# Softmax numerators of every other pair on ScalarE in two batches, mixing tiles of 25 tokens, and an emptier last drain

## The chip, the cores and the metric

One Trainium2 chip, one of its cores. The metric is device time in microseconds of one execution of the kernel; less is better. The numbers of the profile come from one profiled execution of the same kernel.

## The reference

Sixteen batches of x (256 channels, 2048 positions) and a context of the same shape, all in fp32. First a linear attention across channels, then a hyper-connection block; both add to x.

```
qh = softmax over the 64 of each head (Wq @ layernorm(x)) * SCALE       # 8 heads of 64
kh = softmax over positions (Wk @ ctx);  vh = Wv @ ctx
out = Wo @ ((kh @ vh^T)^T @ qh) + bo
x  = x + out / norm(out) * g * sqrt(DIM)

logits = rms_norm(layernorm(x)) @ [W_res, W_pre, W_post]^T + base       # per token, 16 + 4 + 4
H_res  = sinkhorn(logits_res, 50 iterations, tau 0.1), mixed with the identity by a gate
H_pre, H_post = softmax(...)
y = (sum of the 4 streams by H_pre) @ W_branch
x = x + H_res applied to the 4 streams of 512 columns + H_post * y
```

A token is one of the 256 channels of a batch, 2048 wide, cut into four streams of 512.

## The kernel before

Five engines run programs written out by hand, with semaphores. A batch b has a **key stage**, 32 places ("A" or "B", b, r, i) for four blocks r of 128 key rows and four quarters i of the positions, and a **query stage**, places ("Q", b, i) with i from 0 to 26 (STEPS = 27). The query stage works on 16 tiles of 128 positions, in 8 pairs. PE makes a tile's logits in `big[i % 2]` (`query_logits`, L675 to L677); DVE takes each head's maximum (`query_max`, L949) and subtracts it into `q_sb` (`query_subtract`, L959); two steps later ScalarE takes the exponential of the pair (`query_exp`, L1259), POOL adds the halves of each head (`query_half`, L1507, into `x_pre`), DVE sums them and takes the reciprocal (`query_sum`, L967 and L971), and POOL normalises (`query_normalise`, L1515). PE transposes (`query_transpose`, L686, into one of two banks `tb`), ScalarE copies (`turn`, L1254, into one of three `turned`), PE multiplies (`attention_out`, L701). Squares of the result (ScalarE, L1270), its norm (POOL, L1525 and L1528), the scaling (DVE, L980) and the addition to x (POOL, L1535) follow; PE returns the pair to rows (`return_pair`, L720, and the maps of the second block's logits, L723), ScalarE copies the rows (`rows_of_pair`, L1277), DVE takes statistics (L889). `query_logits` of tile i+2 waits until tile i has been read out of `big` (`s_qsub`). Steps 16 to 26 are the drain: no logits of that batch are left, and where another batch follows, its first key logits are made there. Behind the last batch stands one place TAIL.

A **planner** at the top of the file puts further tasks at these places. The batches form five groups (2, 4, 4, 4, 2). When a group's logits are there, its Sinkhorn iteration runs in 116 steps ("sink"), of some three small DVE operations each (L1055 to L1063) with ScalarE's exponentials and logarithms (L1341) between some of them; each step is put at one of the free places of the following batches. For group 3 fewer places than steps are left, so that many places get two. Then the coefficients go to DRAM, and the group's tokens are **mixed** in tiles of TOK = 24 tokens: SP loads 5 rows of 512 columns a token (four streams and y, `mix_ld`, L544), the coefficients (`mix_co`, L546) and biases (L548); POOL (in the last group DVE) builds a block matrix (`mix_w`, L1497, L1133); PE multiplies (L757, two matmul records a tile); ScalarE copies out (`mix_bank`, L1322, two buffers `mix_out`), SP stores 4 rows a token (L554). Loads run four tiles ahead (AHEAD), and one tile is put at every third place (PACE) from the time that its group is ready. What is left goes to TAIL, between the steps of the last group's iteration, and behind that the last group's own tiles, while its last 256 tokens are computed from SBUF (`own`, L1327, L1149, stored by L560 in eight transfers of 128 rows). On each engine, a task waits behind everything put before it.

## Time and profile before

| | |
|---|---|
| median of 3 runs | 2565.55 us (2563.75 to 2566.59) |
| profiled execution | 2568.32 us |
| its span, first to last instruction | 2566.6 us |
| mean granted TensorE clock | 0.982 |
| PE, DVE, ACT, POOL busy | 2413.9, 1726.8, 1172.8, 1094.4 us |
| DMA | 255.72 MB, 100 GB/s in the mean |

In the rows below, engines are PE (TensorE's matmuls), PEld (its weight loads), DVE, ACT (ScalarE), POOL (GpSimd) and SP, which issues the DMAs. A row of a group of instructions has: line, engine, operation, output<-inputs, output shape<-input shape, xcount | busy us, mean ns of one | idle time of the engine just before them and what ended it. Batch 15's query stage begins at 2320.6 us with its first logits, its last logits at 2381.7; the iteration of the last group begins at 2426.8.

### The profile page before, as it was taken

What the parts mean: (1) busy time and instruction counts of PE and PEld (TensorE: products, weight loads), DVE (VectorE), ACT (ScalarE), POOL (GpSimd) and SP (SyncE); (2) the same over time, 40 slices, a digit from 0 to 9 for tenths busy, and PEclk for the clock granted to TensorE, in tenths of its full rate; (3) what the DMA queues carried; (4) which work ended last, traced back from release to release, by engine and by line L of the source; (5) the groups of instructions that cost most, each with busy time, mean ns of one, the idle gap of its engine ahead of it and who ended that gap; (6) DMA issues with size and microseconds to landing.
All of it is one profiled execution on the core that took longest, in us unless ns stands there. A gap on an engine that the chain in (4) does not pass through costs nothing.

```text
span 2566.6 us, 35379 instructions
## 1 busy us (share of the span) xinstructions
PE 2413.9 (94%) x12004; PEld 1914.3 (75%) x12004; DVE 1726.8 (67%) x4114; ACT 1172.8 (46%) x2464; POOL 1094.4 (43%) x1107
## 2 busy tenths in 40 slices
PE   7999999999999999999999999999999999899774
PEld 6888878887878778787877778777778876777521
DVE  4454567676767557776776567667687756877786
ACT  4454444545354444545444454544445344453333
POOL 1635536172635427262543616245272633623410
PEclk9999999999999999999999999999999999999887
DMA  7112221313122432312213243343302233231376
GB/s 237 50 66 99 74 92 56 108 41 103 63 70 96 128 119 83 113 62 70 95 67 99 80 153 93 120 141 101 123 34 90 92 114 117 76 117 44 88 221 193
DMA packets 200145, 255.72 MB, mean 100 GB/s; under 512 B 43550, under 2 KB 109854, under 8 KB 199966
## 3 DMA queue, kind: packets, MB, share of 16 engines
q1 hardware_dynamic: 199966, 253.47, 31.3%
q8 instruction: 96, 1.57, 0.3%
q14 instruction: 83, 0.68, 0.1%
HBM read 177.53 MB, written 75.89 MB: 99 GB/s over the span
## 4 chain that ended last, share of the span: by engine, by line
PE 57%; DVE 20%; POOL 11%; issue 8%; ACT 3%; SPq 1%; DMA 1%; DVEq 0%; POOLq 0%; ACTq 0%
PE kc_bank L642 15%; PE big L701 7%; PE tb L743 4%; PE tb L757 3%; PE tb L628 3%; PE big L616 3%; PE big L618 3%; PE big L617 3%; POOL x_tr L1535 3%; DVE stats L889 3%; PE big L675 3%; PE big L677 2%; PE big L676 2%; PE tb L686 2%; POOL q_sb L1515 2%
## 5 line engine op out<-in xcount | busy, mean ns | idle before, releaser
L1254 ACT COPY turned<-tb 128x512 f32<-128x512 f32 x512 | 298.7, 587 | 755.3 <-PE tb L686 487.9
L701 PE MATMUL big<-merged,turned 128*128 128x256 f32 x2048 | 495.0, 385 | 36.3 <-ACT turned L1254 24.5
L642 PE MATMUL kc_bank<-ctxt,turned 128*128 128x256 f32 x2048 | 479.5, 380 | 3.0 <-DMA ctxt<-in_ctx_t 3.0
L701 PEld LDWEIGHTS big<-merged,turned 128*128 128x128 f32 x2048 | 385.8, 191 | 110.7 <-ACT turned L1254 19.4
L642 PEld LDWEIGHTS kc_bank<-ctxt,turned 128*128 128x128 f32 x2048 | 374.6, 191 | 54.6 <-issue 8.9
L1490 POOL TENSOR_TENSOR in_l<-x_sb,in_h 128x512 fp32r<-128x512 f32 x128 | 167.8, 1340 | 574.9 <-ACT in_h L1294 574.8
L1515 POOL TENSOR_TENSOR q_sb<-q_sb,qsum 128x1024 f32<-128x1024 f32 x128 | 243.8, 1904 | 274.4 <-DVE qsum L971 274.4
L980 DVE SCALAR_TENSOR_TENSOR on<-big,nrm,g_rows 128x256 f32<-128x256 f32 x256 | 111.9, 479 | 220.7 <-POOL nrm L1528 220.4
L616 PE MATMUL big<-in_h,wk_h 128*128 128x512 f32 x512 | 237.7, 464 | 15.4 <-DVE in_l L821 10.0
L675 PE MATMUL big<-wq_h,in_h 128*128 128x512 f32 x512 | 236.4, 462 | 10.9 <-DVE q_sb L959 10.4
L757 PE MATMUL tb<-mix_ld,mix_w 121*96 121x512 f32 (+2 forms) x324 | 187.9, 677 | 57.7 <-POOL mix_w L1497 28.0
L949 DVE TENSOR_REDUCE qmax<-big 128x8 f32<-128x512 f32 x256 | 176.3, 689 | 93.1 <-PE big L677 88.5
L862 DVE TENSOR_REDUCE kmax<-big 128x1 f32<-128x512 f32 x256 | 172.4, 686 | 91.9 <-PE big L618 88.6
L617 PE MATMUL big<-in_l,wk_h 128*128 128x512 f32 x512 | 203.8, 398 | 0.0
L618 PE MATMUL big<-in_h,wk_l 128*128 128x512 f32 x512 | 203.6, 398 | 0.0
L677 PE MATMUL big<-wq_h,in_l 128*128 128x512 f32 x512 | 202.2, 395 | 0.0
L676 PE MATMUL big<-wq_l,in_h 128*128 128x512 f32 x512 | 201.9, 394 | 0.0
L1322 ACT COPY mix_out<-tb 96x512 f32<-96x512 f32 (+2 forms) x162 | 94.0, 580 | 234.4 <-PE tb L757 189.5
L1245 ACT ACTIVATE k_exp<-big,kmax 128x512 f32<-128x512 f32 x256 | 175.4, 689 | 35.5 <-DVE kmax L869 35.4
L959 DVE TENSOR_TENSOR q_sb<-big,qmax 128x512 f32<-128x512 f32 x256 | 169.4, 662 | 28.4 <-PE tb L686 25.8
L889 DVE BATCH_NORM_STATS2 stats<-x_sb 128x6 f32<-128x512 f32 x256 | 163.5, 681 | 35.4 <-ACT x_sb L1277 28.8
L1507 POOL TENSOR_TENSOR x_pre<-q_sb 128x512 f32<-128x512 f32 x128 | 163.0, 1273 | 50.3 <-ACT q_sb L1259 50.1
(149 smaller groups left out, 4308.5 us busy)
## 6 DMA issues: line engine op xcount, KB each, us to landing
mix_ld<-streams SPq DMA_DIRECT2D x157, 240.0 KB
ctxt<-in_ctx_t SPq DMA_DIRECT2D x64, 512.0 KB, 4.0
x_sb<-in_x SPq DMA_DIRECT2D x64, 512.0 KB, 6.1
x_tr<-in_x_t SPq DMA_DIRECT2D x64, 512.0 KB, 6.6
streams<-x_sb SPq DMA_DIRECT2D x64, 512.0 KB, 3.1
stage<-in_ctx SPq DMA_DIRECT2D x60, 512.0 KB, 4.1
out<-mix_out SPq DMA_DIRECT2D x157, 192.0 KB, 2.2
streams<-y_sb SPq DMA_DIRECT2D x32, 256.0 KB, 2.0
```

The source lines that it names most:

```text
L616: nc.tensor.matmul(big[i], wk_h[:, ct, cols], in_h[:, ct, quarter(i)], start=ct == 0, stop=False)
L617: nc.tensor.matmul(big[i], wk_h[:, ct, cols], in_l[:, ct, quarter(i)], start=False, stop=False)
L618: t = nc.tensor.matmul(big[i], wk_l[:, ct, cols], in_h[:, ct, quarter(i)], start=False, stop=ct == CT - 1)
L642: t = nc.tensor.matmul(kc_bank[:, 0:C], turned[n % 3][:, j * P:(j + 1) * P], ctxt[:, nt, :], start=nt == 0, stop=nt == NT - 1)
L675: nc.tensor.matmul(big[i % 2], in_h[:, ct, at], wq_h[:, ct, :], start=ct == 0, stop=False)
L676: nc.tensor.matmul(big[i % 2], in_h[:, ct, at], wq_l[:, ct, :], start=False, stop=False)
L677: t = nc.tensor.matmul(big[i % 2], in_l[:, ct, at], wq_h[:, ct, :], start=False, stop=ct == CT - 1)
L701: t = nc.tensor.matmul(big[2 + p % 2][:, half], turned[n % 3][:, dt * P:(dt + 1) * P], merged[:, dt, :], start=dt == 0, stop=dt == DT - 1)
L757: t = nc.tensor.matmul(bank[0:count * STREAMS, :], weights, mix_ld[k][0:ONES + 1, :], start=True, stop=True)
L889: t = nc.vector.bn_stats(target[:, ct, i, :], x_sb[b % 2][:, ct, quarter(i)])
L1254: nc.scalar.copy(turned[k % 3][:], tb[n % 2][:]).then_inc(s_tba, 1)
L1515: nc.gpsimd.tensor_tensor(exps, exps, qsum[:, p % 2, 1, :].unsqueeze(2).broadcast_to([P, 2 * HEADS, DIM_HEAD]), ALU.mult).then_inc(s_qn, 1)
```

## The change

- SCALAR_PAIRS marks every second pair (1, 3, 5, 7) of batches 14 and 15. For these DVE writes the negated maximum (`qneg`), there is no subtraction, no `query_exp` and no `query_half`. Instead ScalarE's `query_soft` takes, head by head, the exponential of 64 columns straight from `big` with the maximum as bias and the sum as accumulator output, in the step of the tile itself. Waits are rewritten to count the two kinds of pairs.
- TOK is 25, so tiles have 125 and 100 rows.
- Group 3's iteration may not use places behind step 11 of batch 15.
- No mixing tile is put at steps 14 and later of batch 15.
- In steps 16 and later of batch 15 PE transposes a tile before `attention_out` of the one ahead of it, not behind it.

```diff
-    TOK = 24
+    TOK = 25
     PARTS = STREAMS + 1
...
     for gr in range(LAST):
-        free = [place for place in order_of_places[starts[gr]:starts[gr + 1] - 8]
+        free = [place for place in order_of_places[starts[gr]:starts[gr + 1] - (8 if gr < LAST - 1 else STEPS - 12)]
                 if place[0] == "Q" and 5 <= place[2] < NT + 4 or place[0] == "B" and (place[2] >= 2 or place[2:] > (1, 1))
...
             since = min(since, PACE - 6)
-        if place[0] != "Q" and place[2] == 0:
+        if place[0] != "Q" and place[2] == 0 or place[:2] == ("Q", NB - 1) and place[2] >= NT - 2:
             continue
...
     use_tb_behind(TAIL)
+    SCALAR_PAIRS = [b >= FIRST[-1] and k % 2 == 1 for b in range(NB) for k in range(PAIRS)]
+    def scalar_pairs(n):
+        return sum(SCALAR_PAIRS[:n])
+    def vector_pairs(n):
+        return n - scalar_pairs(n)
+    def sums_done(n):
+        return 2 * (n + 1) - scalar_pairs(n + 1)
...
         qmax = sb("qmax", [P, 2, HEADS])
+        qneg = sb("qneg", [P, 2, HEADS])
         qhalf = x_pre[:].rearrange("p (h d) -> p h d", d=DIM_HEAD // 2)
...
             return ap.bitcast(F32)
+        def wait_tile(w, m):
+            n = m // 2
+            if SCALAR_PAIRS[n]:
+                w.wait_ge(s_qacc, 2 * scalar_pairs(n) + m % 2 + 1)
+            else:
+                w.wait_ge(s_qsub, 2 * vector_pairs(n) + m % 2 + 1)
...
                     if b and i < 2:
-                        w.wait_ge(s_qsub, (b - 1) * NT + NT - 1 + i)
+                        wait_tile(w, b * NT - 2 + i)
                     elif b:
...
                 if i >= 2:
-                    w.wait_ge(s_qsub, n - 1)
+                    wait_tile(w, n - 2)
                 else:
...
                         key_context(b, DT - 1, 2 * i + 1)
+                    first = b == NB - 1 and i >= NT
+                    if 4 <= i < NT + 4 and first:
+                        query_transpose(b, i - 4)
                     if 5 <= i < NT + 5:
...
                         return_pair(b, (i - 10) // 2)
-                    if 4 <= i < NT + 4:
+                    if 4 <= i < NT + 4 and not first:
                         query_transpose(b, i - 4)
...
                 w.wait_ge(s_ql, b * NT + i + 1)
+                n = b * PAIRS + i // 2
+                if SCALAR_PAIRS[n]:
+                    w.wait_ge(s_qacc, 2 * scalar_pairs(n))
+                    nc.vector.tensor_reduce(qneg[:, i % 2, :], big[i % 2].rearrange(heads, d=DIM_HEAD), AX_X,
+                                            ALU.max, negate=True).then_inc(s_qmax, 1)
+                    return
                 nc.vector.tensor_reduce(qmax[:, i % 2, :], big[i % 2].rearrange(heads, d=DIM_HEAD), AX_X,
...
                 p = b * PAIRS + i // 2
+                if SCALAR_PAIRS[p]:
+                    return
                 w.wait_ge(s_qmax, n + 1)
...
                 n = b * PAIRS + p
-                w.wait_ge(s_half, n + 1)
-                nc.vector.tensor_reduce(qsum[:, p % 2, 0, :], qhalf, AX_X, ALU.add).then_inc(s_qsum, 1)
-                w.wait_ge(s_qsum, 2 * n + 1)
+                if SCALAR_PAIRS[n]:
+                    w.wait_ge(s_qacc, 2 * scalar_pairs(n + 1))
+                else:
+                    w.wait_ge(s_half, vector_pairs(n + 1))
+                    nc.vector.tensor_reduce(qsum[:, p % 2, 0, :], qhalf, AX_X, ALU.add).then_inc(s_qsum, 1)
+                    w.wait_ge(s_qsum, sums_done(n) - 1)
                 if n >= 2:
...
                 n = b * PAIRS + p
-                w.wait_ge(s_qsub, 2 * n + 2)
+                w.wait_ge(s_qsub, 2 * vector_pairs(n + 1))
                 nc.scalar.activation(q_sb[n % QB][:], q_sb[n % QB][:], ACT.Exp).then_inc(s_qexp, 1)
+            def query_soft(b, i):
+                p, j = i // 2, i % 2
+                n = b * PAIRS + p
+                w.wait_ge(s_qmax, b * NT + i + 1)
+                if p >= QB or b:
+                    last = (n - QB) * 2 + 1
+                    w.wait_ge(s_tb, TB["fg", last // NT * FG + DT * NQ + last % NT] + 1)
+                if n >= 2:
+                    w.wait_ge(s_qsum, sums_done(n - 2))
+                for h in range(HEADS):
+                    cols = slice(h * DIM_HEAD, (h + 1) * DIM_HEAD)
+                    k = j * HEADS + h
+                    t = nc.scalar.activation(q_sb[n % QB][:, j, cols], big[j][:, cols], ACT.Exp, bias=qneg[:, j, h:h + 1],
+                                             accum_out=qsum[:, p % 2, 0, k:k + 1])
+                t.then_inc(s_qacc, 1)
...
                         turn(b * FG + DT * NQ - 1)
-                    if i >= 2 and i % 2 == 0 and i < NT + 2:
+                    if i < NT and SCALAR_PAIRS[b * PAIRS + i // 2]:
+                        query_soft(b, i)
+                    if i >= 2 and i % 2 == 0 and i < NT + 2 and not SCALAR_PAIRS[b * PAIRS + (i - 2) // 2]:
                         query_exp(b, (i - 2) // 2)
...
                 exps = q_sb[n % QB].rearrange("p t (h d) -> p (t h) d", d=DIM_HEAD)
-                w.wait_ge(s_qexp, n + 1)
+                w.wait_ge(s_qexp, vector_pairs(n + 1))
                 if n:
-                    w.wait_ge(s_qsum, 2 * n - 1)
+                    w.wait_ge(s_qsum, sums_done(n - 1))
                 nc.gpsimd.tensor_tensor(qhalf, exps[:, :, 0:DIM_HEAD // 2], exps[:, :, DIM_HEAD // 2:DIM_HEAD],
...
                 exps = q_sb[n % QB].rearrange("p t (h d) -> p (t h) d", d=DIM_HEAD)
-                w.wait_ge(s_qsum, 2 * n + 2)
-                w.wait_ge(s_half, n + 1)
+                w.wait_ge(s_qsum, sums_done(n))
+                w.wait_ge(s_half, vector_pairs(n + 1))
                 nc.gpsimd.tensor_tensor(exps, exps,
...
                         query_normalise(b, (i - 3) // 2)
-                    if i >= 2 and i % 2 == 0 and i < NT + 2:
+                    if i >= 2 and i % 2 == 0 and i < NT + 2 and not SCALAR_PAIRS[b * PAIRS + (i - 2) // 2]:
                         query_half(b, (i - 2) // 2)
```

## Rows read from the trace of the kernel before

**Rows 1.** The page, busy time: us (share of the span) xinstructions.

```profile
PE 2413.9 (94%) x12004; PEld 1914.3 (75%) x12004; DVE 1726.8 (67%) x4114; ACT 1172.8 (46%) x2464; POOL 1094.4 (43%) x1107
```

**Rows 2.** Stretches: keys 10, 14; queries 11, 14, 15; drain 15; iteration; the rest.

```profile
core 0: us, PE busy (x) PEld busy (x) DVE busy (x) ACT busy (x) POOL busy (x), PEclk, DMA share, GB/s
1434.90:1534.10 99.20, 95.08 (x478) 73.75 (x475) 54.94 (x140) 52.44 (x114) 37.82 (x46) 1.00 0.44 136
2045.60:2152.10 106.50, 96.69 (x476) 73.27 (x475) 68.43 (x182) 53.27 (x118) 37.05 (x46) 1.00 0.39 122
1690.40:1748.20 57.80, 57.19 (x287) 46.89 (x286) 40.92 (x78) 23.80 (x48) 34.96 (x32) 1.00 0.33 99
2152.10:2214.70 62.60, 58.73 (x288) 46.82 (x286) 48.49 (x99) 23.79 (x45) 31.77 (x30) 1.00 0.34 103
2320.60:2381.70 61.10, 58.93 (x288) 46.89 (x286) 46.70 (x96) 21.68 (x46) 26.66 (x26) 1.00 0.17 50
2381.70:2426.80 45.10, 35.23 (x167) 26.51 (x168) 29.77 (x69) 14.51 (x37) 23.13 (x29) 0.82 0.23 67
2426.80:2527.90 101.10, 72.55 (x122) 19.35 (x120) 81.50 (x341) 36.55 (x83) 16.58 (x46) 0.82 0.75 212
2527.90:2566.60 38.70, 14.79 (x22) 4.08 (x22) 24.21 (x46) 12.63 (x21) 0.00 (x0) 0.68 0.64 182
```

**Rows 3.** The chain of waits inside batch 15's query stage: start us, us, what.

```profile
by line: DVE skw L1061 16.5%; DVE skw L1055 14.7%; DVE q_sb L959 13.8%; DVE qmax L949 11.0%; issue 7.2%; PE big L675 5.7%; DVE skb L1063 5.6%; DVE ska L1057 5.6%; DVE qsum L967 5.3%; DVE skr L1056 4.6%; DVE skr L1062 4.6%; PE big L677 3.7%;
...
2353.25 1.60 DVE skw L1061
```

**Rows 4.** Groups of instructions by line, the whole span.

```profile
L757 PE MATMUL tb<-mix_ld,mix_w 121*96 121x512 f32 (+2 forms) x324 | 187.9, 677 | 57.7 <-POOL mix_w L1497 28.0 <-DVE mix_w L1133 17.8 <-ACT mix_out L1322 8.0
...
L959 DVE TENSOR_TENSOR q_sb<-big,qmax 128x512 f32<-128x512 f32 x256 | 169.4, 662 | 28.4 <-PE tb L686 25.8
...
L1259 ACT ACTIVATE q_sb<-q_sb 128x1024 f32<-128x1024 f32 x128 | 135.7, 1060 | 104.0 <-DVE q_sb L959 103.9
...
L1270 ACT ACTIVATE squares<-big 128x256 bf16<-128x256 f32 x256 | 98.3, 384 | 24.6 <-PE big L701 20.5
...
L967 DVE TENSOR_REDUCE qsum<-x_pre 128x16 f32<-128x512 f32 x128 | 86.9, 679 | 14.6 <-POOL x_pre L1507 14.3
...
L1270 ACT ACTIVATION_READ_ACCUMULATOR squares<-big 128x1 f32 x256 | 50.6, 198 | 0.0
...
L1341 ACT ACTIVATE skr<-ska 128x32 f32<-128x32 f32 (+1 forms) x25 | 5.7, 226 | 22.1 <-DVE skb L1063 22.1
```

**Rows 5.** The chain of waits at the end of batch 15's drain.

```profile
2419.30 1.84 PE tb L757 x2
...
2421.65 0.59 ACT x_sb L1277
```

**Rows 6.** DMA packets in 2338:2346 us, then in 1012:1020 us with issues.

```profile
DMA packets 384, 0.44 MB, mean 56 GB/s; under 512 B 168, under 2 KB 168, under 8 KB 384
...
DMA packets 487, 0.82 MB, mean 103 GB/s; under 512 B 94, under 2 KB 94, under 8 KB 486
...
streams<-x_sb SPq DMA_DIRECT2D x1, 512.0 KB, 2.9
...
mix_ld<-streams SPq DMA_DIRECT2D x1, 80.0 KB
```

**Rows 7.** DMA packets and issues in the tail, 2480:2520 us.

```profile
DMA packets 8321, 9.83 MB, mean 246 GB/s; under 512 B 3557, under 2 KB 3557, under 8 KB 8318
...
q1 hardware_dynamic: 8318, 9.80, 86.5%
...
mix_ld<-streams SPq DMA_DIRECT2D x21, 240.0 KB
```

**Rows 8.** DMA packets in 2340.87:2341.19 us, one engine at work.

```profile
DMA packets 5, 0.01 MB, mean 26 GB/s; under 512 B 1, under 2 KB 1, under 8 KB 5
```

**Rows 9.** ScalarE in the tail, in order of time.

```profile
2496.97 0.58 ACT L1322 COPY mix_out<-tb 96x512 f32<-96x512 f32 x1 [1.28 <-DMA out<-mix_out]
```

More of the change, by code:

```diff
@@ L293, in xattn_ffn @@
         s_qsub = sem("s_qsub")
+        s_qacc = sem("s_qacc")
         s_qexp = sem("s_qexp")
```

## The prediction, before the changed kernel was run

> **What bounds the kernel now.** I read the page's busy times first: PE is busy for 94% of the span [rows 1], so most of the kernel is a matter of what PE is given to do. Then the stretches by stage [rows 2], where the reader is to compare like with like. The query stage of batch 11 takes 57.8 us with PE busy for 57.2 of them; those of batches 14 and 15, with the same PE instructions to within one, take 62.6 and 61.1 us. What differs is DVE: 48.5 and 46.7 us busy against 40.9. The chain of waits inside batch 15 runs through DVE for most of its length, Sinkhorn products ahead of all, one of them at 1.60 us [rows 3]. So there DVE sets the pace. The drain of batch 15 (45.1 us) is a mixture, and its last link is a mixing tile: ScalarE's copy of the returned rows comes behind a matmul of L757 [rows 5]. From there to the end of the iteration of the last group (101.1 us) two things run side by side. DVE is busy for 81.5 us; the DMA engines are busy for 75%, and at 86.5% in the stretch of [rows 7], where 40 us hold 21 tile loads, so 1.9 us a tile. ScalarE's copy out waits there for the DMA of two tiles before [rows 9]. That stretch is bound by DVE and by the transfers at once, which matters for what follows. The last 38.7 us are transfers and the eleven last tiles.
>
> **Mixing tiles of 25: count.** Groups of 512, 1024 and 256 tokens give 22, 43, 43, 43 and 11 tiles of 24, and 21, 41, 41, 41 and 11 of 25: 155 instead of 162. Followed through the planner, three of the seven saved lie in key stages (one in batch 7, two in batch 12), three in the last batch, and one behind the last batch (49 instead of 50 under the last group's iteration). A tile's two matmuls cost PE 0.86 us at the full clock in the chain (their 677 ns each [rows 4] overlap): -2.6 us for the three.
>
> **Mixing tiles of 25: the transfers.** A load has 5 rows of 2 KB a token, 120 before and 125 after, a store 4 rows a token, 96 and 100. How rows are shared out is to be read from the small packets. In the first stretch of [rows 6] one store of 96 rows, one load of 120, one load of 120 coefficient rows and one bias row leave 168 packets under 512 B: 120 coefficients, 1 bias, and 47 others. In the second the load has 40 rows (80 KB): 94 small packets, less 40 and 1 leaves 53, with a spill of 128-row form beside it. Taken as one closing packet from each DMA engine that took part, 47 is 16+15+15+1 and 53 is 16+16+10+10+1. So 96 rows went over 16 engines, 120 over 15, 40 over 10: each time the largest number up to 16 that divides the rows. 125 is 5x5x5, so I forecast five engines for each load, and ten for a store of 100 rows. The Trainium skill, in DMA: Bandwidth & Descriptors, section "Why a DMA increments its semaphore by 16 and not by 1", states that very rule for the engine count, and also that such a transfer goes to the lowest-numbered engines; the trace agrees on the counts (47 and 53), and no row shows which engines. This speaks against the change.
>
> The price. On its own, one DMA engine moved four 2 KB packets in 0.32 us [rows 8], 0.080 us each. In the loaded tail 8318-3557 = 4761 large packets kept 86.5% of 16 engines busy over 40 us, 0.116 us each with all small ones put on them [rows 7]. An engine that takes part in both has 8+6 = 14 large packets a tile now, 1.1 to 1.6 us of the 1.9. With the change the busiest five have 25+10 = 35: 2.8 us at the lower price, 4.1 at the upper. I take 0.095 us, 3.3 us a tile, since what makes a packet dearer than 0.080 comes in part once a transfer, and a transfer now has more packets. 49 tiles: 163 us, against 101.1 us: **+62 us** (137 to 201: +36 to +100). DVE's iteration is hidden behind it, but its last ScalarE functions are queued behind the copies out of all 49 tiles, so the last group's coefficients come that much later. In the last 38.7 us the eleven tiles put about 11x35x0.095 = 37 us on the busiest engines and the eight stores of the last tokens (128 rows, 8 packets each) 6 us more, from the first load, which comes once the coefficients are stored, some 5 us in by my estimate: 48 to 50 us, **+11 us** (+5 to +21).
>
> Before the last batch a tile comes every third place, some 12 us apart (57.8 us for 15 places [rows 2]), and is loaded four tiles ahead, so 35 packets (3.3 us) an engine are covered; only other loads queued behind four first loads of a group (10 us) can be late. I take +2 us (0 to +8).
>
> **Every other pair by ScalarE.** In batches 14 and 15 four pairs each lose on DVE two subtractions of 662 ns and one sum of 679 ns [rows 4], 2.0 us, and on POOL a half sum. ScalarE loses one exponential of 1.06 us and gains sixteen of 64 columns with sixteen accumulator reads of 198 ns. Nearest rows for the former: 226 ns for 32 columns, 384 for 256. So a head costs from 0.20 us (the activation hidden under the read) to 0.58, and I take 0.226+0.198 = 0.43, since 64 is nearest to 32: 3.4 us a tile, 6.9 a pair. ScalarE is busy for 23.8 of 62.6 us in this stage [rows 2], 3 us a pair of about 9: with 5.8 more it has 9 in such a pair and 3 in the next. It fits, but not freely. The exponential of the pair before is now queued behind the first tile's eight heads, so POOL's half sum and DVE's next sum come some 3 us later: I estimate 1.5 us of the 2.0 saved are lost to that wait. What is next late is PE, whose floor for the stage is batch 11's 57.8 us: at most -4.8 and -3.3 us.
>
> **The iteration of group 3** has 116 steps; its places end at step 11 of batch 15 instead of 18. So batch 14 gets 35 instead of 31 in its key stage and 32 instead of 28 in its query stage, batch 15 gets 34 instead of 31 and then 15 instead of 28. In key stages 15 more steps cost 106.5-99.2 = 7.3 us [rows 2], 0.49 each: 7 more, +3.5 us (0 to +7; DVE is busy 13.5 us more for the 15 steps, 0.9 a step). In batch 14's query stage four more steps eat what DVE is saved: -1 us (-4.8 to +5); in batch 15's -2 us (-3.3 to +4).
>
> **The last drain.** Thirteen steps at 0.9 us leave DVE, three mixing tiles leave PE, and a transpose goes ahead of the product that waits for ScalarE's copy of the transpose before. In all but one short stretch after the last product the order of PE sets the end. The link through L757 goes wholly: the rows can be copied when PE is done with the maps, at 2419.3 instead of 2421.65 [rows 5], 2.3 us. PE is idle for 10 of the 45.1 us and runs at 0.82 of its clock, its lower level for part of it [rows 2]. I take -8 us (0 to -13).
>
> **Sum**, against the profiled execution of 2568.3 us (span 2566.6, 1.7 around it): -2.6 +62 +11 +2 +3.5 -1 -2 -8 = +65. The median of the runs is 2.8 us under the profiled one: 2565.55+65 = **2630 us**. All lower ends together give about +15, all upper ones about +140.
>
> **Rivals.** (1) The transfers spread evenly after all, since 125 rows are shared some other way or each transfer starts at another engine. For it: no row shows a number without a divisor between 6 and 16, nor which engines are used. Against: 15 for 120 and 10 for 40 are what divisors give, and an even share would have given 16 and 14 or more. A tile then costs as now, one tile less lies in the tail, and -2.6+3.5-1-2-8 = -10 remains: **2555 us**, faster. It decides as soon as the busiest engine has fewer than 1.9/0.095 = 20 packets a tile. (2) The same, with ScalarE as the bound of the two query stages: at 0.7 us a head (the 0.58 above and a wait of 0.12) a pair would be 11 us on top of 2, against 9 of PE: +4 us on eight pairs, 2555+35 = **2590 us**. For it: accumulator reads are separate instructions; against: durations of neighbours on one engine mostly overlap, and it takes the far end of the price. (3) The five engines bind, but at their floor of 0.080 us and with the drain at its best: still about 2582 us, part of the forecast.
>
> **How the numbers follow.** Forecast 0.86, rival 1 0.09, rival 2 alone 0.05. Of the forecast only its lowest corner could be under +0.2% (what a measurement can tell apart here is about 0.2%, 5 us): 0.01. Slower 0.85+0.04 = 0.89, same 0.01+0.01+0.01 = 0.03, faster 0.08. The range leaves rival 1 out (0.09) and a few hundredths at each end of the forecast: 2592 to 2685 us.
>
> **What would show it.** In the tail, GB/s falls from 246 to near 130 to 150, with the DMA share near half; ScalarE's and POOL's waits for DMA grow; DVE, now over 80% busy there, falls to near 50%. A step with one tile has 16-byte packets 125 instead of 120 and 10+5+5+1 = 21 closing packets. Query stages of 14 and 15 near 60 us; copies of rows in the last drain without a mixing copy ahead. The prediction is wrong if the tail's 49 tiles still pass at 1.9 us each.

## The result

The changed kernel takes 2614.2 us (median, 2613.8 to 2614.5), the kernel before beside it 2564.65 us: ratio 1.0191, interval 1.0175 to 1.0207. It is 49.6 us slower. The forecast was 2630 us, with a range of 2592 to 2685.

The page of the kernel after: busy times, and the last three rows of the 40 slices (65.3 us each).

```profile
PE 2431.3 (93%) x11990; PEld 1915.5 (73%) x11990; DVE 1703.7 (65%) x4090; ACT 1200.0 (46%) x2705; POOL 1083.6 (41%) x1092
...
PEclk9999999999999999999999999999999999999655
DMA  7112122213132342213123442433212342311444
GB/s 233 57 62 101 65 97 73 89 46 112 46 100 79 121 140 96 89 41 113 49 67 97 129 140 87 150 92 103 93 65 97 102 131 85 115 50 44 145 158 156
```

PE is busy for 93% (94% before), and for 17 us more in all. In the last three slices the granted clock is 0.6, 0.5 and 0.5 of full speed, and the DMA share is 0.4 to 0.5. PE at a low clock and partly idle, the DMA engines more than half idle, and yet the stretch is long: something narrow sets it.

The stretches of the kernel after that answer to [rows 2]: the query stage of batch 14, the stretch to batch 15's, its query stage, its drain, the last group's iteration, the rest.

```profile
core 0: us, PE busy (x) PEld busy (x) DVE busy (x) ACT busy (x) POOL busy (x), PEclk, DMA share, GB/s
...
2147.40:2212.40 65.00, 59.07 (x288) 46.67 (x287) 43.09 (x93) 34.91 (x141) 28.61 (x27) 1.00 0.30 93
2212.40:2325.30 112.90, 98.89 (x480) 75.03 (x478) 87.87 (x235) 57.13 (x148) 37.55 (x46) 0.98 0.28 89
2325.30:2390.40 65.10, 59.11 (x288) 46.62 (x287) 38.99 (x90) 32.03 (x138) 25.62 (x25) 1.00 0.16 44
2390.40:2425.10 34.70, 28.37 (x164) 23.60 (x163) 12.74 (x32) 16.51 (x62) 18.11 (x23) 0.90 0.16 57
2425.10:2568.00 142.90, 94.28 (x120) 23.42 (x118) 81.82 (x344) 37.02 (x82) 16.77 (x45) 0.60 0.45 154
2568.00:2612.50 44.50, 19.82 (x22) 4.67 (x22) 23.93 (x44) 12.19 (x19) 0.00 (x0) 0.57 0.47 159
```

| stretch | before | after | difference |
|---|---|---|---|
| up to batch 14's query stage | 2152.1 | 2147.4 | -4.7 |
| query stage of batch 14 | 62.6 | 65.0 | +2.4 |
| from there to batch 15's query stage | 105.9 | 112.9 | +7.0 |
| query stage of batch 15 | 61.1 | 65.1 | +4.0 |
| drain of batch 15 | 45.1 | 34.7 | -10.4 |
| iteration and rest | 139.8 | 187.4 | +47.6 |

The differences sum to +45.9, that of the spans. The before column is worked out from [rows 2] and the times between them; 105.9 is 2320.6 less 2214.7. The iteration and the rest stand together here, since their border is an operation's end; by the end of DVE's last coefficient operation they are 101.8 and 38.0 before, 142.9 and 44.5 after. The reader is to see in the iteration's row that DVE is busy for the same 82 us as before, ScalarE for the same 37, and that the DMA share fell from 0.75 to 0.45: only PE is busy for longer, at a clock of 0.60 instead of 0.82, and by the chain below it does not set the end (its matmuls of tiles are 5.2% of that chain).

The chain of waits of the kernel after, from the start of the iteration to the end (2425 to 2612 us): its shares by line, and three of its pieces (start us, us, what).

```profile
by line: DMA out<-mix_out 62.4%; ACT mix_out L1377 8.2%; DMA mix_w<-bias_rows 7.1%; PE tb L781 5.2%; DVE k_exp L1187 5.2%; issue 2.7%; SPq L570 1.4%; SPq L572 1.0%; SPq L568 0.6%; ACT k_exp L1382 0.4%; ACT skp L1396 0.4%; SPq L578 0.4%; DVE
...
2442.16 0.59 ACT mix_out L1377
2442.77 4.89 DMA out<-mix_out
2447.74 0.59 ACT mix_out L1377
```

62% of the chain is stores of mixed tiles on their way, 4.89 us in the piece shown. Under the iteration ScalarE waits 41 times for such a store, 89.2 us in all; in the kernel before it was 28 times and 33.8 us, of which [rows 9] shows one. From a copy over its store to the next copy but one, which needs the same buffer, it is 5.6 us for two tiles here, and 142.9 us for 49 in the mean, 2.92 each.

### The profile page after: what moved, and what is told of

It reads as the page before. It is cut to its first block, busy times and chain, and to the rows that moved or that the text cites. A ratio compares the mean times of both kernels' runs of the same rounds, so it can differ in the third digit from the quotient of the medians.

```text
span 2612.5 us, 35500 instructions
## 1 busy us (share of the span) xinstructions
PE 2431.3 (93%) x11990; PEld 1915.5 (73%) x11990; DVE 1703.7 (65%) x4090; ACT 1200.0 (46%) x2705; POOL 1083.6 (41%) x1092
## 4 chain that ended last, share of the span: by engine, by line
PE 56%; DVE 16%; POOL 10%; issue 7%; DMA 5%; ACT 4%; SPq 1%; POOLq 0%; DVEq 0%; ACTq 0%
PE kc_bank L666 15%; PE big L725 8%; DMA out<-mix_out 4%; PE tb L767 4%; PE tb L652 3%; PE big L640 3%; PE big L642 3%; PE big L641 3%; PE tb L781 3%; POOL x_tr L1592 3%; DVE stats L916 2%; PE big L699 2%; PE big L701 2%; PE big L700 2%; PE tb L710 2%
## 5 line engine op out<-in xcount | busy, mean ns | idle before, releaser
L781 PE MATMUL tb<-mix_ld,mix_w 126*100 126x512 f32 (+2 forms) x310 | 206.3, 759 | 82.8 <-POOL mix_w L1554 51.5
L982 DVE TENSOR_REDUCE qmax<-big 128x8 f32<-128x512 f32 x240 | 165.0, 688 | 95.0 <-PE big L701 90.8
L1377 ACT COPY mix_out<-tb 100x512 f32<-100x512 f32 (+1 forms) x155 | 90.9, 587 | 265.3 <-PE tb L781 157.9
L1564 POOL TENSOR_TENSOR x_pre<-q_sb 128x512 f32<-128x512 f32 x120 | 152.7, 1273 | 84.7 <-ACT q_sb L1297 84.5
L1592 POOL TENSOR_TENSOR x_tr<-x_tr,on 128x512 f32<-128x512 f32 x128 | 164.9, 1288 | 39.7 <-DVE on L1018 39.7
```

Of the source, the lines that this page charges most:

```text
L781: t = nc.tensor.matmul(bank[0:count * STREAMS, :], weights, mix_ld[k][0:ONES + 1, :], start=True, stop=True)
L1592: nc.gpsimd.tensor_tensor(pair, pair, on[:], ALU.add).then_inc(s_sum, 1)
```

## How the transfers are shared out

One tile in the body of the kernel after, 2343:2351 us, which answers to [rows 6].

```profile
GB/s 0 0 0 0 143 102 113 113 143 174 102 92 82 123 133 123 133 123 133 123 133 123 67 35 42 0 1 0 0 0 0 0 0 0 0 0 0 0 0 0
DMA packets 373, 0.47 MB, mean 59 GB/s; under 512 B 147, under 2 KB 147, under 8 KB 372
...
mix_ld<-streams SPq DMA_DIRECT2D x1, 250.0 KB
```

147 packets under 512 B: 125 coefficient rows, one bias row, and 21 others. Read as closing packets, 21 is 10 for the store of 100 rows, 5 for the load, 5 for the coefficients and 1 for the bias row. That is what the divisors gave. With the load alone at work the rate is 123 to 133 GB/s in slice after slice (0.2 us each), five times the 26 GB/s of one engine in [rows 8].

### Tiles of 25 and nothing else: e1_tok25

```diff
-    TOK = 24
+    TOK = 25
```

> The kernel before with tiles of 25 tokens and nothing else. Theory 1 (a load of 125 rows goes over five DMA engines, 25+10 packets of 2 KB a tile on the busiest): the 50 or so tiles behind the last batch pass at 2.9 us each as in the changed kernel, against 1.9; the iteration of the last group takes about 143 to 150 us instead of 101, the end 6 us more, so 2608 to 2618 us in all, nearly the whole of what the change cost. Rival (the slower tail comes from the other edits, which leave more to do there): within 10 us of the kernel before.

Measured: 2603.86 us, ratio 1.0138 (1.0123 to 1.0153). The iteration and the rest:

```profile
2418.30:2554.70 136.40, 88.44 (x114) 21.57 (x112) 81.75 (x344) 35.24 (x79) 15.99 (x43) 0.61 0.45 153
2554.70:2599.70 45.00, 18.98 (x22) 4.28 (x22) 23.88 (x44) 12.19 (x19) 0.00 (x0) 0.62 0.47 158
```

136.4+45.0 = 181.4 us instead of 139.8, so 41.6 us of the changed kernel's 47.6. The iteration and the total are 7 and 4 us under the ranges I had written: with the old planning only 46 tiles are left for the iteration, not 49, and 46 at 2.97 us is 136.4. The other three are those that the changed kernel takes out of the last batch. The loss of the tail comes with this one number; the rival falls.

### Five rows apart: e5_split_load

The changed kernel; a tile's semaphore is waited for at 64 instead of 48.

```diff
-                nc.sync.dma_start(mix_ld[k][0:count * PARTS, :], streams[tokens].rearrange("c s n -> (c s) n")).then_inc(
-                    s_mixld[k], 16)
+                for part in (slice(0, count - 1), slice(count - 1, count)):
+                    nc.sync.dma_start(mix_ld[k][part.start * PARTS:part.stop * PARTS, :],
+                                      streams[first + part.start:first + part.stop].rearrange("c s n -> (c s) n")
+                                      ).then_inc(s_mixld[k], 16)
```

> The changed kernel, tiles of 25, but each tile's load is issued as two DMAs: the rows of all its tokens but the last (120 rows) and those of the last (5 rows). Same bytes, one issue more a tile. Theory 1 (engines are shared out by divisors of the rows, always from the same end): 8+1 rows of the load and 10 of the store, 19 packets at most an engine instead of 35, 1.6 us, so that SP's five issues a tile (1.9 us) or DVE's iteration set the pace: the last iteration takes 100 to 108 us instead of 142.9, 2565 to 2578 us in all. Rival (tiles of 25 are slow in the tail for another reason: more bytes in one load, 25 columns blocks for POOL, waits in SP): 135 us or more, and no faster than the changed kernel.

Measured: 2578.09 us, ratio 1.0045 (1.0032 to 1.0059), 36 us under the changed kernel for the same bytes. The iteration:

```profile
2427.00:2538.00 111.00, 78.37 (x120) 20.00 (x118) 82.26 (x344) 36.52 (x81) 16.48 (x45) 0.76 0.68 197
```

111.0 us, 2.27 a tile, 3 us over the upper end I gave; the total is at its upper end. One tile's issues on SP in that kernel, from a store to the next:

```profile
2494.38 0.29 SPq L580 DMA_DIRECT2D out<-mix_out  x1
2494.71 0.68 SPq L569 DMA_DIRECT2D mix_ld<-streams  x2
2495.44 0.42 SPq L572 DMA_DIRECT2D mix_co<-coef_rows  x1
2495.91 0.48 SPq L574 DMA_DIRECT2D mix_w<-bias_rows  x1
2496.43 0.29 SPq L580 DMA_DIRECT2D out<-mix_out  x1
```

SP is taken for 2.05 us a tile by five issues. I had put them at 1.9. That is close to the 2.27, but SP still waits 25.7 us in this stretch for ScalarE's copies, so it does not set the pace alone; what sets the rest was not tried. That the load on five engines was the cause is shown: the same rows as 120 and 5 pass in 111.0 us, as 125 in 142.9.

### Tiles of 23: e6_tok23

```diff
-    TOK = 24
+    TOK = 23
```

> The kernel before with tiles of 23 tokens and nothing else: 115 rows in (divisors 5 and 23) and 92 out (4 and 23). 54 tiles under the last iteration instead of 50. Theory 1 (fixed engines, from the same end): 23+23 = 46 packets a tile on the busiest four, at 0.083 us 3.8 us a tile; the iteration takes 195 to 215 us, the kernel 2670 to 2700. Theory 1b (the divisor rule, but loads and stores on different engines): 23 packets, 1.9 us a tile, 103 to 112 us, 2570 to 2585. Rival (a tile's size decides, and 23 is smaller than 24): as before, within 12 us.

Measured: 2686.95 us (one execution with its profile), 121 us over the kernel before, by a tile that is one token smaller. The iteration:

```profile
2429.10:2629.20 200.10, 110.75 (x130) 24.32 (x128) 81.48 (x344) 39.41 (x87) 17.87 (x51) 0.55 0.32 112
```

200.1 us for 54 tiles, 3.71 us a tile; with 23+23 packets that is 0.081 us a packet. This run was chosen for the question that no row before could answer: which engines. 115 rows go over five and 92 over four: one tile in its body (2340 to 2348 us) leaves 131 packets under 512 B, 115 coefficients, one bias row and 15 others, which are 5+4+5+1. Had loads and stores used different ones, or another set each time, the busiest would have had 23 packets or fewer and the iteration some 105 us, by an estimate from 1.9 us a tile. So both go to the same ones each time. The Trainium skill says the same in DMA: Bandwidth & Descriptors, section "Why a DMA increments its semaphore by 16 and not by 1": the lowest-numbered engines. The runs agree in that the sets overlap (46 packets at 0.081 us, not 23); that they are the lowest is not shown here.

Four kernels side by side, with the busiest engine's packets of 2 KB a tile:

| kernel | packets | us a tile | us a packet |
|---|---|---|---|
| before, tiles of 24 | 8+6 = 14 | 1.9 | 0.14 (not the limit alone) |
| e5, 120+5 in, 100 out | 8+1+10 = 19 | 2.27 | 0.12 (not the limit alone) |
| after, 125 in, 100 out | 25+10 = 35 | 2.92 | 0.083 |
| e6, 115 in, 92 out | 23+23 = 46 | 3.71 | 0.081 |

The last two have nearly the price of an engine on its own, 0.080 us [rows 8]; e1, with the same 35 packets, has 2.97 us a tile and 0.085.

## What the other edits do

### All but the tile size: e2_after_tok24

```diff
-    TOK = 25
+    TOK = 24
```

against the changed kernel.

> The changed kernel with tiles of 24 tokens. Theory 1: the iteration is back at about 102 us and the rest at 38; what stays is the query stages and the key stage of the last two batches (+1 +2 +7 +4 us) against the drain (-10), so 2566 to 2572 us. Rival (the edits themselves weigh on the tail, since the tiles taken out of the last batch have to be mixed there): iteration over 108 us, total over 2578.

Measured: 2572.81 us, ratio 1.0021 (1.0012 to 1.0031). The same stretches but the first and the last (batch 14's queries, to batch 15's, its queries, drain, iteration):

```profile
2149.10:2214.10 65.00, 60.11 (x288) 48.00 (x287) 43.14 (x93) 34.86 (x141) 28.61 (x27) 0.97 0.31 96
2214.10:2329.80 115.70, 101.73 (x478) 77.18 (x477) 87.84 (x235) 56.96 (x148) 37.33 (x46) 0.96 0.28 86
2329.80:2394.90 65.10, 59.14 (x288) 46.63 (x287) 39.01 (x90) 32.02 (x138) 25.59 (x25) 1.00 0.16 43
2394.90:2429.80 34.90, 28.56 (x164) 23.80 (x163) 12.73 (x32) 16.52 (x62) 18.12 (x24) 0.89 0.20 57
2429.80:2533.40 103.60, 74.53 (x128) 19.57 (x126) 82.13 (x344) 38.98 (x86) 17.36 (x49) 0.84 0.78 219
```

The iteration is back at 103.6 us, with 53 tiles in it where the kernel before has 50; the total is 0.8 us over the range I had given. The rest of the change is a small loss of its own, since the drain's gain is spent ahead of it: 115.7 and 65.1 us where it was 105.9 and 61.1.

### Without the pairs: e3_no_pairs

```diff
-    SCALAR_PAIRS = [b >= FIRST[-1] and k % 2 == 1 for b in range(NB) for k in range(PAIRS)]
+    SCALAR_PAIRS = [False for b in range(NB) for k in range(PAIRS)]
```

against e2_after_tok24.

> The changed kernel with tiles of 24 tokens and no pair on ScalarE: what is left is the emptier last drain and the denser iteration of group 3. Theory 2 (a tile's 2.4 us on ScalarE stand between DVE's maximum and the release of its logit bank, so a late DVE costs PE more than the 2.0 us a pair that DVE is saved): the query stages of batches 14 and 15 are faster than in the changed kernel, 62 to 64 us and 60 to 62 against 65.0 and 65.1; total 2557 to 2564 us. Rival (the stages are slower since the iteration is denser, 32 steps for 28): the stages stay at 65 or get worse, since DVE is saved nothing, total over 2570.

Measured: 2566.34 us, ratio 0.9996 (0.9986 to 1.0005), 2 us over the range I had given.

```profile
2150.80:2214.70 63.90, 59.09 (x288) 46.85 (x286) 50.13 (x102) 24.49 (x49) 31.77 (x30) 1.00 0.33 103
2214.70:2328.70 114.00, 102.79 (x477) 77.37 (x477) 90.54 (x238) 53.14 (x116) 39.11 (x47) 0.96 0.27 82
2328.70:2389.70 61.00, 58.27 (x289) 46.77 (x287) 46.12 (x99) 21.09 (x45) 28.11 (x27) 1.00 0.18 46
2389.70:2422.60 32.90, 26.98 (x164) 22.57 (x162) 14.65 (x35) 12.82 (x31) 20.47 (x25) 0.93 0.17 60
```

The query stages are 63.9 and 61.0 us, in the ranges written. But the stretch between them is still 114.0, with DVE busy for 90.5 us (83.5 before), so theory 2 does not explain that one; the denser iteration was left.

### The pairs alone: e4_pairs_only

The kernel before with the pairs; free places, mixing and the order in the drain as they were. Against the changed kernel, with TOK = 24 besides:

```diff
-        free = [place for place in order_of_places[starts[gr]:starts[gr + 1] - (8 if gr < LAST - 1 else STEPS - 12)]
+        free = [place for place in order_of_places[starts[gr]:starts[gr + 1] - 8]
...
-        if place[0] != "Q" and place[2] == 0 or place[:2] == ("Q", NB - 1) and place[2] >= NT - 2:
+        if place[0] != "Q" and place[2] == 0:
...
-                    first = b == NB - 1 and i >= NT
+                    first = False
```

> The kernel before with every other pair of batches 14 and 15 on ScalarE and nothing else (tiles of 24, drain and iteration as before). Theory 2: the query stages of 14 and 15 take 63 to 66 us against 62.6 and 61.1, so 2566 to 2572 us. Rival (DVE was the bound, each marked pair gives it 2.0 us, and the denser iteration took the gain in the changed kernel): 58 to 60 us each, total 2557 to 2562 us.

Measured: 2566.94 us, ratio 0.9996 (0.9985 to 1.0007): no difference in the total.

```profile
2152.30:2215.50 63.20, 59.08 (x288) 46.66 (x287) 43.08 (x91) 33.98 (x137) 29.60 (x28) 1.00 0.32 98
2319.80:2381.90 62.10, 58.37 (x289) 46.89 (x287) 40.10 (x87) 32.02 (x138) 23.96 (x23) 1.00 0.15 44
```

63.2 and 62.0 us (the second row's window is 0.1 longer), with DVE busy for 43.1 and 40.1 us instead of 48.5 and 46.7. Batch 15's stage is 1 us under the range I had written. 5 to 7 us of DVE's time are gone from each stage, and the stages are not shorter. A part comes out elsewhere: in this profile the stretch between the two stages is 104.3 us instead of 105.9 and the drain 42.6 instead of 45.1, so that from batch 14's first logits to the iteration it is 272.1 us instead of 274.7. The medians do not tell these 2.6 us from nothing. Two things take the place of what DVE is saved in the stages, to be seen in the changed kernel. First, who waited in its query stage of batch 14 (us in total, times, longest):

```profile
POOL x_pre L1564 <- ACT q_sb L1297: 16.4, 3, 7.5
...
PEld big L699 <- ACT q_sb L1312: 7.8, 5, 3.2
...
DVE qsum L1005 <- POOL x_pre L1564: 5.3, 2, 3.1
```

DVE waits 5.3 us for POOL's half sum, and POOL 16.4 us for ScalarE's exponential of the vector pair before, which stands behind eight heads. PE's loads of weights wait 7.8 us for ScalarE to read the logits out of the bank. And one such place in order of time:

```profile
2194.72 0.69 DVE L979 TENSOR_REDUCE qneg<-big 128x8 f32<-128x512 f32 x1
...
2195.44 0.31 ACT L1312 ACTIVATE q_sb<-big,qneg 128x64 f32<-128x64 f32 x1 [4.81 <-DVE qneg L979]
2195.65 0.19 ACT L1312 ACTIVATION_READ_ACCUMULATOR q_sb<-big,qneg 128x1 f32 x1
2195.75 0.30 ACT L1312 ACTIVATE q_sb<-big,qneg 128x64 f32<-128x64 f32 x1
...
2197.77 1.09 ACT L1297 ACTIVATE q_sb<-q_sb 128x1024 f32<-128x1024 f32 x1
...
2197.97 0.50 PE L699 MATMUL big<-wq_h,in_h 128*128 128x512 f32 x1 [2.97 <-ACT q_sb L1312]
```

DVE comes late to the tile (2194.72), 0.7 us later ScalarE starts, and each head takes 0.29 us from start to start. After 2.3 us the last is read, and PE goes on at 2197.97. Before, DVE's subtraction would have let it go on 0.7 us after the maximum. A late DVE is made 1.6 us later.

### The drain, and the iteration: e7_mix_and_turn and e8_dense_only

e7 is e3_no_pairs with group 3's iteration at its old places:

```diff
-        free = [place for place in order_of_places[starts[gr]:starts[gr + 1] - (8 if gr < LAST - 1 else STEPS - 12)]
+        free = [place for place in order_of_places[starts[gr]:starts[gr + 1] - 8]
```

> Tiles of 24, no pair on ScalarE, iteration of group 3 placed as before; only no mixing tile from step 14 of the last batch, and the transpose ahead of the product in the last drain. Theory 3 (what the emptier drain wins, the denser iteration loses in the stretch before batch 15's query stage): query and key stages as before (62.6, 106, 61), drain 38 to 43 us, iteration 102 to 105, total 2558 to 2563 us. Rival (the drain is short only since the iteration left it): drain 44 to 46, within 2 us of the kernel before.

Measured: 2562.03 us, ratio 0.9984 (0.9976 to 0.9993). The stretch to batch 15's query stage, and the drain:

```profile
2212.00:2319.50 107.50, 99.96 (x475) 76.50 (x476) 83.52 (x223) 52.53 (x116) 39.62 (x47) 0.97 0.29 89
2380.60:2420.20 39.60, 29.52 (x161) 24.59 (x162) 29.73 (x70) 12.64 (x34) 22.10 (x26) 0.85 0.14 43
```

e8 is the kernel before with that one edit the other way round:

```diff
-        free = [place for place in order_of_places[starts[gr]:starts[gr + 1] - 8]
+        free = [place for place in order_of_places[starts[gr]:starts[gr + 1] - (8 if gr < LAST - 1 else STEPS - 12)]
```

> The kernel before with group 3's iteration ended at step 11 of batch 15 and nothing else. Theory 3: the stretch from batch 14's last logits to batch 15's first takes 112 to 116 us instead of 105.9 and its query stage 1 to 2 us more, the drain 36 to 41 instead of 45.1: 2565 to 2573 us. Rival (the 8 us in that stretch come from other edits): 106 to 108 there, and 2555 to 2561 us.

Measured: 2567.55 us, ratio 1.0006 (0.9997 to 1.0016). The same two stretches:

```profile
2215.50:2327.70 112.20, 99.30 (x477) 74.87 (x477) 90.52 (x238) 52.99 (x116) 39.03 (x47) 0.98 0.29 87
...
2388.70:2427.70 39.00, 33.53 (x173) 25.12 (x171) 14.51 (x36) 14.83 (x35) 21.45 (x28) 0.91 0.31 96
```

and in the kernel before, for the first of them:

```profile
2214.70:2320.60 105.90, 98.36 (x475) 75.14 (x476) 83.49 (x223) 52.57 (x116) 39.62 (x47) 0.98 0.30 90
```

Each shortens the drain by about 6 us (39.6 and 39.0 instead of 45.1), but e8 pays them back ahead of it: 112.2 us instead of 105.9, DVE busy for 90.5 us instead of 83.5. Five steps more lie in that stretch (9 instead of 7 in the drain of batch 14, 34 instead of 31 among the keys), so 1.3 us a step. Batch 14's query stage with its two steps more is 63.9 us, 1.3 over the kernel before; batch 15's is 61.0, where I had expected 1 to 2 us more. Theory 3 holds. e7 has two edits of the drain together, no late mixing tile and the transpose first; what each is worth was not tried.

### The pairs once more: e9, e10 and e11

e9 is the changed kernel with tiles of 24 and the old places of the iteration.

> The changed kernel with tiles of 24 and group 3's iteration at its old places (pairs on ScalarE, no late mixing tile, transpose first). Theory 2 (pairs on ScalarE win DVE 2.0 us and lose about as much in the waits for the bank and for the half sum): as the same kernel without pairs, 2560 to 2564 us, query stages 62 to 64 us each, drain 1 to 3 us shorter than its 39.6. Rival (the pairs were only spoilt by the denser iteration and pay with the old one): query stages under 60, total 2552 to 2558 us.

Measured: 2562.92 us, ratio 0.9982 (0.9973 to 0.9991), as e7 without pairs (0.9984); query stages 63.2 and 62.0 us, drain 37.9. The rival falls: the denser iteration was not what spoilt the pairs.

e10 puts the exponential first:

```diff
-                    if i < NT and SCALAR_PAIRS[b * PAIRS + i // 2]:
-                        query_soft(b, i)
                     if i >= 2 and i % 2 == 0 and i < NT + 2 and not SCALAR_PAIRS[b * PAIRS + (i - 2) // 2]:
                         query_exp(b, (i - 2) // 2)
+                    if i < NT and SCALAR_PAIRS[b * PAIRS + i // 2]:
+                        query_soft(b, i)
```

> The same with one more edit: on ScalarE the exponential of the vector pair before is put ahead of the first tile's eight heads, not behind them. Theory 2: DVE's waits for POOL's half sum (5.3 us in batch 14's query stage) and POOL's for the exponential (13.9) mostly go, but the first tile's heads come 1.1 us later where ScalarE is late; query stages 1 to 3 us shorter, 2556 to 2562 us. Rival (only the release of the logit bank counts, and that comes later by the exponential): query stages equal or up to 3 us longer, 2562 to 2568 us.

Measured: 2556.55 us, ratio 0.9959 (0.9945 to 0.9972). Its stretches from batch 14's query stage to the end of the drain, and the waits in the first of them:

```profile
2152.30:2213.00 60.70, 58.53 (x287) 46.80 (x286) 43.52 (x91) 34.10 (x137) 29.52 (x28) 1.00 0.31 94
2213.00:2319.00 106.00, 98.23 (x478) 75.21 (x477) 80.53 (x219) 56.60 (x148) 36.68 (x45) 0.98 0.31 93
2319.00:2380.40 61.40, 58.39 (x289) 47.01 (x287) 41.49 (x89) 32.37 (x138) 25.04 (x24) 1.00 0.15 44
2380.40:2416.70 36.30, 28.81 (x164) 23.90 (x163) 25.05 (x64) 17.04 (x66) 18.68 (x24) 0.88 0.18 57
```

```profile
POOL q_sb L1572 <- DVE qsum L1009: 20.8, 6, 5.1
...
PEld big L699 <- ACT q_sb L1312: 3.8, 4, 1.2
```

The query stage of batch 14 is 60.7 us instead of e9's 63.2. POOL's waits for the exponential fell from 13.9 us in e9 to 2.1, and DVE's for the half sum (5.3) are no longer among the view's longest; what POOL waits for now is DVE's sum, 20.8 us instead of 12.0. The loads' wait for the bank fell too, from 5.9 to 3.8 us. So the order on ScalarE was a large part of the pairs' price; how the 2.5 us divide between the half sum and the bank is not shown, since one edit moved both. And 1.7 us of them are handed back: the stretch behind the stage is 106.0 us, where e9's profile has 104.3. From batch 14's first logits to the iteration e10 takes 264.4 us and e9 267.4. The medians of the two are 6.4 us apart, and their intervals only just do not meet (e9 from 0.9973 on, e10 up to 0.9972), so a gain is shown, but its size only roughly. This is the fastest kernel of the study, together with e12 below, 0.4% under the kernel before.

e11 is e10 with pairs in batch 15 alone (`b >= NB - 1`).

> The same with pairs on ScalarE in the last batch alone. Theory 2: batch 14's query stage returns to 62.6 us and the stretch behind it to about 106; what the pairs win in the last drain stays: 2556 to 2561 us, at or under both its neighbours. Rival (pairs win in batch 14 as well, since DVE's backlog is carried into the key stage): 1 to 3 us slower than with both batches.

Measured: 2560.29 us, ratio 0.9970 (0.9961 to 0.9980); batch 14's query stage 62.6 us again. With the right order the pairs are worth 2 us in batch 14's stage. The medians are 3.7 us apart, with intervals that overlap; the rival was right.

### 25 in the first three groups, 24 in the last two: e12_25_then_24

e10 with

```diff
-    TOK = 24
+    TOK = 25
...
-    MIX_TILES = [[(FIRST[n] * C + at, min(TOK, size * C - at)) for at in range(0, size * C, TOK)]
+    STEP = (25, 25, 25, 24, 24)
+    MIX_TILES = [[(FIRST[n] * C + at, min(STEP[n], size * C - at)) for at in range(0, size * C, STEP[n])]
```

> The kernel of e10_exp_first with tiles of 25 tokens in the first three groups, which are mixed three places apart in the body, and of 24 in the last two, which are mixed behind the last batch. 5 tiles fewer in the body. Theory 1: 35 packets on the busiest engine every 12 us are hidden, so the five tiles' 0.86 us of PE each are won and the iteration stays at 104 us: 4 us less than e10, 2550 to 2555 us. Rival (five-engine loads also delay other transfers in the body, or the tiles saved there were hidden): 2556 to 2562 us.

Measured: 2556.65 us (2553.0 to 2557.9), ratio 0.9966 (0.9952 to 0.9979), no different from e10. That is in the rival's range and over mine, and my count was wrong: by the planner only three of the five tiles saved leave the body. The other two leave the tail, and the last seven tiles of 25 tokens are mixed there: of ScalarE's 51 copies of tiles from 2408 us on seven have 100 rows. The iteration is 104.3 us for its 51 tiles, e10's 103.9 for 53, so there nothing is won; with the seven at 2.92 us and the others at 1.9 it would be 104, by an estimate.

In the body the loads over five engines reach POOL and not PE. From 500 to 2140 us POOL waits 25.2 us for the transfers of tiles (12.9 in e10), but PE waits for POOL's matrices 4.6 us in three places, 4.5 in e10. So this part of the rival, loads that delay the others there, is not borne out. Whether the three tiles are worth their 2.6 us in the body stays open: the time at which batch 14's query stage begins differs by 5 us between profiles of kernels whose program up to there is the same (2147.5 us in e9, 2152.3 in e10).

## Why the prediction was right, and where it was off

**The transfers.** The step that carried the forecast, five engines for 125 rows and ten for 100, always the same ones, is borne out by the closing packets (21), by e1, e5 and e6. The size was off: forecast +62 and +11 us, together +73, measured +47.6. The term that was mis-sized is the price of a packet. I took 0.095 us, between 0.080 of [rows 8] and 0.116 of [rows 7]; on the busiest engines it is 0.083. The mean over all engines, worked out as in [rows 7], is another figure:

```profile
DMA packets 10126, 12.73 MB, mean 159 GB/s; under 512 B 3964, under 2 KB 3964, under 8 KB 10121
...
q1 hardware_dynamic: 10121, 12.68, 45.7%
```

These are 2460 to 2540 us of the kernel after: 10121-3964 = 6157 large packets and 45.7% of 16 engines over 80 us, 0.095 us each. That happens to be what I took, but the pace follows the busiest engines alone, and these are at the floor. Why the mean fell from 0.116 was not tried; nearly all engines were at work at once there, and about half of them here.

49 tiles at 35x0.083 = 2.9 us are 142 us, and the eleven last tiles with 35x0.083 each, 32 us, the eight stores' 5 us and the 5 us before the first load are 42 us against 44.5 measured. With the measured price the forecast would have been 2602 us, 12 us under the result instead of 16 over it. Of these 12, 3 us are only that the profiled execution before lies above its median, and 9 are the query stages; the other terms nearly cancel. So the middle of the range was met as closely as it was in part by luck: a tail forecast too dear and query stages forecast too cheap.

Two sums of the prediction do not come out. Its own 48 to 50 us for the last stretch are 9 to 11 us more than 38.7, so +11 is their upper end; and at 0.080 us a packet the same terms give some 2 us more, not the +5 of its lower end. And rival 3, the floor of 0.080 with the drain at its best, gives about 2593 us; 2582 takes every term at its lower end.

**The body.** Three tiles, -2.6 us, against -4.7 up to batch 14's query stage; within what equal programs differ by there. The +2 us for late loads did not come in the body: from 500 to 2140 us POOL waits 24.8 us for tiles instead of 12.8, and PE for POOL's matrices 4.6 us in both kernels.

**The query stages.** Forecast -1 and -2 us, measured +2.4 and +4.0: wrong in sign. The 2.0 us that a pair saves on DVE were right (DVE busy 43.1 and 39.0 us instead of 48.5 and 46.7; in batch 14's stage there are six subtractions and three sums fewer, 6.0 us for three pairs). The price of a head, 0.43 us, was too high: 0.29. And a pair lasts 62.6/8 = 7.8 us, not the 9 that I set against ScalarE's work. What failed is the step to the stage. I counted the exponential behind the heads as 1.5 of the 2.0 us, and said that PE would be next at 57.8 us. I left out that the bank is released by ScalarE 2.3 us after the maximum instead of 0.7, and that PE waits for it. By e10 the order was worth 2.5 us in batch 14's stage, of which the stretch behind it gave back 1.7.

**The iteration.** Forecast +3.5 us for seven more steps in the two key stages. The first four cost nothing that can be told (e11 and e12 have 106.5 us for batch 14's key stage without them, e9 and e10 107.9 without them as well, the changed kernel 107.8 with them). The stretch behind batch 14's logits costs 6.3 us (e8), for five steps, not three: I had counted the two in its drain to the query stage, and 0.49 us a step is too little where DVE is busy for 83.5 of 105.9 us already. There the time goes up nearly as DVE's work does, 7.0 us.

**The drain.** Forecast -8 us, measured -10.4; e7 and e8 give about 6 each way, 12.2 both together without the pairs (e3, 32.9 us). The steps were miscounted: before, 26 and not 28 lie behind batch 15's keys, 21 of them at steps up to 15 and only 5 in the drain, so eleven go and not thirteen. That they free DVE in the drain is so all the same, since DVE is late: in e8 it has 36 operations there instead of 69.

**The rivals.** The first, an even spread, is ruled out by e6 and e1. The second asked for 0.7 us a head; it is 0.29. The third had the price of a packet nearly right, with the drain too short. Of the signs named, the DMA share near half came (0.45) and the rate is 154 GB/s against 130 to 150; DVE's share is 0.57.

## What to carry to other kernels

Before a tile's size is changed, divide the rows of its DMAs: in every count read here (128, 125, 120, 115, 100, 96, 92 and 40 rows) the largest divisor up to 16 is how many engines they got, and a count with small primes (120, 96, 128) is worth more than one row more. Where it matters shows only where transfers set the pace: read the small packets of one quiet tile, then price the busiest engine's packets at what one engine does alone. And work that goes from a busy engine to an idle one must be placed by who waits behind it there, or the gain is handed back.

## What was not expected of the hardware

- A tile one token smaller made the kernel 121 us slower (23 instead of 24 tokens), and one token larger 37 us. The number of engines that share the rows does more than the bytes.
- A busiest engine's price of a 2 KB packet is steady at 0.081 to 0.085 us over 200, 143 and 136 us of load (e6, the changed kernel, e1), nearly the 0.080 of four packets alone.
- Short ScalarE activations with an accumulator read follow each other every 0.29 us at 64 columns, although the two instructions' own durations add to 0.5 us (0.31+0.19 in the rows above).
- In the iteration of the changed kernel the granted clock is 0.60 of full speed, its lower level of 1.2 GHz for most of the stretch. It fell at 2418.5 us, behind 5.5 us in which PE was busy for 3.7. It costs little there: a tile's two matmuls take 2.0 us instead of 0.86, and still they are only 5.2% of the chain, since PE waits for the transfers.
